# Moving the even-row copies out of PSUM from VectorE to ScalarE in a transformer block's first residual stage

## The chip, the cores and the metric

The kernel runs on the eight cores of one Trainium2 chip. Each core takes one batch element (2048 rows of 1024 numbers) and there is no communication between the cores. The metric is the device time in microseconds of the slowest core; lower is better.

## The reference

One layer with four layer norms, computed for each of eight batch elements (weights shared, the FFN's weights int32 scaled by 1/127, biases zero in the data but applied):

```python
x = x + layernorm(attention(layernorm(x)))      # 16 heads of 64, causal, 2048 x 2048
x = x + layernorm(ffn(layernorm(x)))            # silu(x Wg) * (x Wu), hidden 3072, then Wd
```

## The kernel before

The work of a core comes in this order. (1) The first layer norm of the 16 row tiles of 128 x 1024, with their transposes. (2) Q, K and V projections and causal attention, the projections fed in between the steps of attention. (3) The output projection, L315, with results held feature-major (128 features x 2048 rows, eight such chunks) in `s_f`; ScalarE evicts them from PSUM, L749. (4) The **row stage**, which the change touches: 16 row tiles go through layer norm, residual add and the next layer norm, and back to feature-major. (5) The gate and up matmuls (L840, L851), then the down matmul (L886). (6) A last stage of layer norms, residual adds and stores to memory, which has the same shape as (4).

A tile j of the row stage passes through four functions:

- `p3_A(j)`: TensorE transposes the eight 128 x 128 blocks of the tile into one PSUM bank, in bf16 (L761); the bank is chosen by j % 2. A copy takes the bank to `s_ln` (L768), again one of two halves by j % 2. Then `emit_ln` normalizes it into `s_at`.
- `p3_B(j)`: GpSimd adds the result to the residual `s_x` (L780).
- `p3_C(j)`: `emit_ln` normalizes the sum; its mean was already found in stage (1), so the first reduction is left out.
- `p3_D(j)`: TensorE transposes that (L800) and ScalarE copies it from PSUM into `s_f` (L808).

`emit_ln` is a chain over two engines. VectorE: sum (L239, `p3_A` only), sum of squares (L245, reads its source twice), two 128 x 1 operations (L250, L253). ScalarE: logarithm and exponential for the reciprocal root (L256, L259). VectorE: one 128 x 1 operation (L262). ScalarE: the normalizing pass over 128 x 1024 (L265).

The loop issues the functions skewed: at step t come A(t), B(t-1), C(t-2), D(t-3). Each engine runs its own operations in the order in which they are issued. On ScalarE, step t is thus L256, L259, L265 of A(t), then the same three of C(t-2), then L808 of D(t-3). On VectorE it is L768, L239, L245, L250, L253, L262 of A(t), then L245, L250, L253, L262 of C(t-2). On TensorE it is the transposes of A(t), then those of D(t-3).

All dependencies are tracked by name and become semaphore waits in `emit_all`: for each operation the engine is given one wait instruction for every dependency whose count is higher than the highest it has already waited for, in ascending order:

```python
for d in sorted(o["deps"]):
    ch, val, _ = ops[d]["token"]
    ...
    wait(ch, val)        # skipped when this engine has waited for val or more
```

L808 of tile j names in `war` all transposes that read the four-tile group of `s_f` into which it writes.

Of the kernel before, what the change touches and what calls it, by code (L numbers as in the profile page):

```python
# [26 lines left out]
class Prog:  # L27
# [11 lines left out]
    def op(self, engine, emit, reads=(), writes=(), queue=None, war=(),  # L39
           deps=(), bump=()):  # L40
        idx = len(self.ops)
        dep = set(deps)
        for r in reads:
            e = self.res.get(r)
            if e is not None and e[0] is not None:
                dep.add(e[0])
        for w in tuple(writes) + tuple(war):
            e = self.res.get(w)
            if e is not None:
                if e[0] is not None:  # L50
                    dep.add(e[0])
                dep |= e[1]
        dep.discard(idx)
        self.ops.append({"engine": engine, "emit": emit, "deps": dep,
                         "queue": queue, "token": None})
        for r in reads:
            self.res.setdefault(r, [None, set()])[1].add(idx)
        for w in writes:
            self.res[w] = [idx, set()]
        for w in bump:  # L60
            self.res.setdefault(w, [None, set()])[0] = idx
        return idx
# [59 lines left out]
def build_program(trunc=0, trunc_step=None):  # L122
# [40 lines left out]
    op = P.op  # L163
# [278 lines left out]
    def emit_v_round(c, si):  # L442
# [48 lines left out]
       writes=["vones"])  # L491
# [249 lines left out]
    for c in range(ND):  # L741
# [5 lines left out]
        for si in range(4):  # L747
# [4 lines left out]
               reads=["ps%d" % si, "bo"], writes=["zf_%d_%d" % (c, si)],  # L752
               war=["xnT%d" % (4 * si + k) for k in range(4)])

    def p3_A(j):
        par = j % 2
        bank1 = "ps%d" % (4 + par)
        pb = pO[:, 512 * par:512 * (par + 1)].bitcast(BF16)
        for c in range(ND):
            op("pe",  # L760
               lambda e, c=c, j=j, pb=pb: e.transpose(  # L761
                   pb[:, 128 * c:128 * (c + 1)],
                   s_f[:, S * c + 128 * j: S * c + 128 * (j + 1)], IDT),
               reads=["zf_%d_%d" % (c, j // 4), "cst"],
               writes=([bank1] if c == 0 else []),
               bump=([] if c == 0 else [bank1]))
        ztm = s_ln[:, 1024 * par:1024 * (par + 1)]
        op("dve", lambda e, pb=pb, ztm=ztm: e.tensor_copy(ztm, pb[:, 0:1024]),  # L768
           reads=[bank1], writes=["lnr%d" % par],
           war=["osc0", "osc1"])  # L770
        yn = s_at[:, 1024 * par:1024 * (par + 1)]
        emit_ln(ztm, "lnr%d" % par, yn, "yn%d" % par, pid=j % 4, eng="dve",
                dst_war=("at0",) if j < 2 else (),
                war0=(["rrq0", "rrq1", "onq0", "onq1"] if j == 0 else ()))
# [37 lines left out]
    for t in range(NJ + 3):  # L812
        if t < NJ:
            p3_A(t)
        if 0 <= t - 1 < NJ:
            p3_B(t - 1)
        if 0 <= t - 2 < NJ:
            p3_C(t - 2)
        if 0 <= t - 3 < NJ:
            p3_D(t - 3)  # L820

    for hc in range(NHC):
# [12 lines left out]
        for si in range(4):  # L835
            for kc in range(ND):
# [7 lines left out]
                   reads=["wb%d" % gslot] + ["ynT%d" % (4 * si + k) for k in range(4)],  # L844
                   writes=(["ps%d" % si] if first else []),
                   bump=([] if first else ["ps%d" % si]))
            for kc in range(ND):
# [7 lines left out]
                   reads=["wb%d" % uslot] + ["ynT%d" % (4 * si + k) for k in range(4)],  # L855
                   writes=(["ps%d" % (4 + si)] if first else []),
# [5 lines left out]
               reads=["ps%d" % si], writes=["silu%d" % (si % 2)],  # L862
               war=(("rrq1", "onq1") if (hc == 0 and si < 2) else ()))
# [4 lines left out]
               reads=["silu%d" % (si % 2), "ps%d" % (4 + si)],  # L868
               writes=["h_%d_%d" % (hc, si)],
               war=hwar if si == 0 else ())  # L870

    for c in range(ND):
# [5 lines left out]
           writes=["wd%d_0" % slot, "wd%d_1" % slot], queue="qpool",  # L878
           war=((["wb4", "wb5", "q20", "q21"]
                 + ["nbrow%d" % c2 for c2 in range(ND)]) if c < 2 else ()))  # L880
        for si in range(4):
            for hc in range(NHC):
# [8 lines left out]
                   reads=["wd%d_%d" % (slot, hc // 12), "h_%d_%d" % (hc, si)],  # L891
                   writes=(["ps%d" % si] if first else []),
# [5 lines left out]
               reads=["ps%d" % si], writes=["df_%d_%d" % (c, si)],  # L898
               war=(ALLYNT if (c == 0 and si == 0) else ()))
# [90 lines left out]
```

How the kernel before makes its waits and increments, by code:

```python
        def body(ename, eng):  # L88
            wm = {}
            def wait(ch, val):
                if wm.get(ch, 0) < val:
                    eng.wait_ge(sems[ch], val)
                    wm[ch] = val
            for i in per_eng[ename]:
                o = ops[i]
                if o["queue"] is not None and i in burst_settle:
                    wait(o["queue"], burst_settle[i])
                for d in sorted(o["deps"]):
                    ch, val, _ = ops[d]["token"]
                    if ops[d]["queue"] is not None:
                        val = burst_end_val[d]
                    wait(ch, val)
                inst = o["emit"](eng)
                if o["token"] is not None:
                    ch, val, inc = o["token"]
                    inst.then_inc(sems[ch], inc)
            if ename == "sp":
                for d in sorted(final_deps):
                    ch, val, _ = ops[d]["token"]
                    wait(ch, val)
```

## Time and profile before

| | us |
|---|---|
| median of three runs | 1689.13 |
| lowest and highest | 1688.15, 1689.35 |
| the profiled execution | 1688.57 |
| span of its slowest core, the one shown | 1687.0 |
| spans of all eight cores | 1681.6 to 1687.0 |
| granted TensorE clock, cores' mean | 0.852 to 0.855 |
| busy in the span: TensorE, ScalarE, VectorE, GpSimd | 1220.9, 668.7, 503.4, 226.3 |

A span runs from a core's first to its last instruction. The profiled execution's own time is 1.57 us longer than the longest span; what lies around the span is taken as fixed. Busy times of the engines overlap, so they say nothing by themselves of what sets the end.

### The profile page before, as it was taken

The page shows a single profiled execution, that of the slowest core. Times are in us where ns is not written, and L with a number is a line of the kernel's source. Part 1 is how long each engine was busy: PE and PEld are TensorE (multiplying, and loading weights), DVE is VectorE, ACT ScalarE, POOL GpSimd, SP SyncE. Part 2 cuts the span into 40 slices and gives each one's busy share as a digit, 9 for nine tenths or more (in the row PEclk, how much of TensorE's full clock was granted, in tenths as well). Part 3 has the DMA queues.
Part 4 walks back from the last instruction along what each step waited for, and adds up shares of the span by engine and source line. Part 5 has one row for each costly group of instructions (what it writes and reads, how often), then busy time and mean ns, then how long its engine had stood idle before and what let it go on. Part 6 is the DMA issues. An engine that isn't in the chain of part 4 may idle for free.

```text
span 1687.0 us, 22179 instructions; the slowest of 8 cores (1681.6 to 1687.0 us)
## 1 busy us (share of the span) xinstructions
PE 1220.9 (72%) x5648; PEld 539.1 (32%) x5648; DVE 503.4 (30%) x1074; ACT 668.7 (40%) x1004; POOL 226.3 (13%) x205
## 2 busy tenths in 40 slices
PE   1447777776767777677776932299999999999910
PEld 0123232232323323223222422144444444444410
DVE  4543233231332313233221057711122111000076
ACT  3243554546445464454665335621111111111154
POOL 5202101010110101001000123311111111000022
PEclk9768798897978979798887965599999999999955
DMA  7402100001010010000000300044443446244222
GB/s 87 54 1 19 13 14 7 10 11 13 13 14 10 4 17 10 1 7 7 10 4 7 32 7 0 6 44 40 38 39 38 38 38 62 21 38 38 19 88 112
DMA packets 114632, 43.49 MB, mean 26 GB/s; under 512 B 109264, under 2 KB 109392, under 8 KB 114512
## 3 DMA queue, kind: packets, MB, share of 16 engines
q0 software_dynamic: 111360, 35.66, 19.8%
q1 hardware_dynamic: 2432, 6.29, 1.1%
q8 instruction: 52, 0.85, 0.2%
q14 instruction: 68, 0.56, 0.1%
q10 hardware_dynamic: 720, 0.13, 0.0%
HBM read 63.05 MB, written 8.39 MB: 42 GB/s over the span
## 4 chain that ended last, share of the span: by engine, by line
PE 63%; DVE 17%; ACT 10%; issue 7%; DMA 2%; POOL 1%; DVEq 0%; ACTq 0%; POOLq 0%
PE pS L840 10%; PE pO L851 10%; PE pS L886 10%; PE pS L623 8%; PE pS L377 8%; PE pO L560 7%; DVE s_dmp L245 5%; ACT s_at L646 5%; PE pS L452 3%; DVE s_dmp L239 3%; PE pS L315 3%; ACT s_dmp L509 2%; ACT pO L505 1%; DVE s_at L461 1%; DVE s_b L390 1%
## 5 line engine op out<-in xcount | busy, mean ns | idle before, releaser
L646 ACT ACTIVATE s_at<-pS,s_nB 128x512 bf16<-128x512 f32 (+4 forms) x521 | 349.1, 707 | 313.2 <-PE pS L631 155.0
L623 PE MATMUL pS<-s_b,s_y 128*128 128x512 bf16 (+3 forms) x640 | 227.7, 402 | 30.0 <-ACT s_at L646 13.3
L560 PE MATMUL pO<-s_at,s_b 128*128 128x512 bf16 (+3 forms) x640 | 194.5, 405 | 12.0 <-ACT s_at L646 6.8
L840 PE MATMUL pS<-s_f,s_wb 128*128 128x512 bf16 x768 | 183.2, 382 | 0.0
L851 PE MATMUL pO<-s_f,s_wb 128*128 128x512 bf16 x768 | 181.6, 379 | 0.0
L886 PE MATMUL pS<-s_b,s_wd 128*128 128x512 bf16 x768 | 165.9, 379 | 0.0
L860 ACT ACTIVATE s_dmp<-pS 128x512 bf16<-128x512 f32 x96 | 57.3, 597 | 270.2 <-PE pS L840 270.2
L865 DVE TENSOR_TENSOR s_b<-s_dmp,pO 128x512 bf16<-128x512 bf16 x96 | 66.0, 688 | 270.6 <-PE pO L851 256.4
L377 PE MATMUL pS<-s_f,s_wb 128*128 128x512 bf16 x384 | 126.3, 433 | 18.7 <-ACT s_f L291 10.6
L329 POOL TENSOR_TENSOR s_wd<-s_b 128x512 bf16<-128x512 bf16 x64 | 66.4, 1038 | 402.8 <-DVE s_b L390 358.7
L623 PEld LDWEIGHTS pS<-s_b,s_y 128*128 128x128 bf16 x640 | 69.6, 110 | 125.7 <-issue 90.4
L840 PEld LDWEIGHTS pS<-s_f,s_wb 128*128 128x128 bf16 x768 | 75.5, 98 | 91.3 <-issue 1.7
L851 PEld LDWEIGHTS pO<-s_f,s_wb 128*128 128x128 bf16 x768 | 75.2, 98 | 91.0 <-issue 0.8
L886 PEld LDWEIGHTS pS<-s_b,s_wd 128*128 128x128 bf16 x768 | 75.1, 98 | 90.6
L501 DVE CAST s_ln<-pO 64x1024 bf16<-64x1024 f32 x32 | 38.9, 1216 | 194.6 <-PE pO L560 194.5
L560 PEld LDWEIGHTS pO<-s_at,s_b 128*128 128x128 bf16 x640 | 61.1, 106 | 108.4 <-issue 78.0
L239 DVE TENSOR_SCALAR_CACHE_REDUCE s_dmp<-s_ln 128x1024 bf16<-128x1024 bf16 x32 | 38.9, 1215 | 168.5 <-ACT s_ln L916 166.6
L514 PE MATMUL pO<-s_dmp,s_cst 1*64 1x512 bf16 x32 | 15.5, 486 | 88.5 <-ACT s_dmp L509 88.5
L800 PE MATMUL pO<-s_cst,s_at 128*128 128x128 bf16 x128 | 16.2, 306 | 86.8 <-ACT s_at L265 86.8
L895 ACT ACTIVATE s_f<-pS 128x512 bf16<-128x512 f32 x32 | 19.1, 597 | 148.4 <-PE pS L886 148.4
L631 PE MATMUL pS<-s_cst 128*128 128x128 bf16 x256 | 63.4, 247 | 0.0
L283 PE MATMUL pO<-s_cst,s_ln 128*128 128x128 bf16 x128 | 15.0, 290 | 64.1 <-ACT s_ln L265 64.1
(91 smaller groups left out, 1230.5 us busy)
## 6 DMA issues: line engine op xcount, KB each, us to landing
s_wb<-wg POOLq DMA_DIRECT2D x24, 256.0 KB, 5.0
s_wb<-wu POOLq DMA_DIRECT2D x24, 256.0 KB, 4.6
s_wd<-wd POOLq DMA_DIRECT2D x8, 768.0 KB, 10.3
s_x<-x POOLq DMA_DIRECT2D x16, 256.0 KB, 7.7
y<-s_y SPq DMA_DIRECT2D x8, 512.0 KB, 2.6
y<-s_y POOLq DMA_DIRECT2D x8, 512.0 KB, 3.0
s_wb<-wq POOLq DMA_DIRECT2D x8, 256.0 KB, 5.5
s_b<-s_dmp SPq DMA_DIRECT2D x16, 128.0 KB, 2.2
```

Of the source, the lines that this page charges most:

```text
L239: op("dve", lambda e, mc=mc: e.tensor_scalar(dmp, src_ap, 1.0 / D, 0.0, ALU.mult, ALU.add, accum_out=mc), reads=[src_res], writes=[mres, " ...
L245: op("dve", lambda e: e.scalar_tensor_tensor(dmp, src_ap, 1.0 / D, src_ap, ALU.mult, ALU.mult, accum_out=cell(3)), reads=[src_res], writes ...
L329: op("pool", lambda e, src_ap=src_ap, q2=q2: e.tensor_mul(q2, src_ap, src_ap), reads=[dres], writes=["q2%d" % par])
L377: e.matmul(out, wslot(slot)[:, 128 * kc:128 * (kc + 1)], xfm(kc)[:, 512 * si:512 * (si + 1)], start=first, stop=(kc == ND - 1), skip_group ...
L560: e.matmul(pO[:, q0:q0 + n], s_b[:, V0 + 1040 * j + 65 * h: V0 + 1040 * j + 65 * h + 128], s_at[:, 2048 * par + (q0 - 128 * j): 2048 * par ...
L623: e.matmul(pS[:, 512 * sl:512 * sl + n], kpadv[hp][:, 128 * ktc:128 * (ktc + 1)], q_fm(c)[:, q0:q0 + n], start=True, stop=(not diag), skip ...
L631: lambda e, sl=sl: e.matmul(pS[:, 512 * sl:512 * sl + 128], NEGI, LMSK, start=False, stop=True, skip_group_check=True),
L646: lambda e, src=src, dst=dst, c=c: e.activation(dst, src, AF.Exp, bias=s_nB[:, c:c + 1], scale=QSCALE),
L840: e.matmul(acc_view(si), wslot(gslot)[:, 128 * kc:128 * (kc + 1)], xfm(kc)[:, 512 * si:512 * (si + 1)], start=first, stop=(kc == ND - 1)),
L851: e.matmul(pO[:, 512 * si:512 * (si + 1)], wslot(uslot)[:, 128 * kc:128 * (kc + 1)], xfm(kc)[:, 512 * si:512 * (si + 1)], start=first, sto ...
L865: lambda e, hc=hc, si=si, stg=stg: e.tensor_tensor(s_b[:, S * hc + 512 * si: S * hc + 512 * (si + 1)], stg, pO[:, 512 * si:512 * (si + 1)] ...
L886: e.matmul(acc_view(si), s_wd[:, 3072 * slot + 128 * hc: 3072 * slot + 128 * (hc + 1)], s_b[:, S * hc + 512 * si: S * hc + 512 * (si + 1)] ...
```

## The change

In `p3_A` the copy from the PSUM bank to `s_ln` is issued on ScalarE for even tiles. For odd tiles it stays on VectorE. The operation stands in the same place of the issue order, with the same source, destination and dependencies.

```diff
         ztm = s_ln[:, 1024 * par:1024 * (par + 1)]
-        op("dve", lambda e, pb=pb, ztm=ztm: e.tensor_copy(ztm, pb[:, 0:1024]),
-           reads=[bank1], writes=["lnr%d" % par],
-           war=["osc0", "osc1"])
+        if par == 0:
+            op("act", lambda e, pb=pb, ztm=ztm: e.copy(ztm, pb[:, 0:1024]),
+               reads=[bank1], writes=["lnr%d" % par],
+               war=["osc0", "osc1"])
+        else:
+            op("dve", lambda e, pb=pb, ztm=ztm: e.tensor_copy(
+                ztm, pb[:, 0:1024]),
+               reads=[bank1], writes=["lnr%d" % par],
+               war=["osc0", "osc1"])
```

## Rows read from the trace of the kernel before

**Rows 1.** The page's first line: the span of the slowest core

```profile
span 1687.0 us, 22179 instructions; the slowest of 8 cores (1681.6 to 1687.0 us)
```

**Rows 2.** Windows of the row stage: us, busy by engine, clock, DMA

```profile
980.00:1000.00 20.00, 2.83 (x34) 2.15 (x32) 15.25 (x30) 6.03 (x12) 5.24 (x3) 0.61 0.00 0
...
1020.00:1040.00 20.00, 5.60 (x48) 4.88 (x48) 14.63 (x37) 11.58 (x21) 6.35 (x3) 0.50 0.00 0
1040.00:1060.00 20.00, 5.59 (x48) 4.88 (x48) 14.87 (x37) 11.91 (x19) 6.35 (x3) 0.50 0.00 1
```

**Rows 3.** Groups by line, row stage: form, count, busy us, mean ns, idle

```profile
L265 ACT ACTIVATE s_at<-s_ln,s_st 128x1024 bf16<-128x1024 bf16 x16 | 19.8, 1240 | 6.6 <-DVE s_st L262 6.6
...
L808 ACT COPY s_f<-pO 128x1024 bf16<-128x1024 bf16 x13 | 12.9, 993 | 0.9 <-PE pO L800 0.9
L768 DVE COPY s_ln<-pO 128x1024 bf16<-128x1024 bf16 x16 | 10.9, 681 | 58.3 <-PE pO L761 58.3
```

**Rows 4.** Timeline around tile 6's copy: start us, length us, operation, idle before

```profile
1016.29 1.06 PE L761 MATMUL pO<-s_cst,s_f 128*128 128x128 bf16 x8
...
1020.06 2.12 POOL L780 TENSOR_TENSOR s_x<-s_x,s_at 128x1024 bf16<-128x1024 bf16 x1 [4.91 <-ACT s_at L265]
...
1020.50 0.20 ACT L259 ACTIVATE s_st<-s_st 128x1 f32<-128x1 f32 x1
1020.80 0.21 DVE L262 TENSOR_SCALAR s_st<-s_sx,s_st 128x1 f32<-128x1 f32 x1 [0.70 <-ACT s_st L259]
1020.93 0.68 DVE L768 COPY s_ln<-pO 128x1024 bf16<-128x1024 bf16 x1
1021.11 1.24 ACT L265 ACTIVATE s_at<-s_x,s_st 128x1024 bf16<-128x1024 bf16 x1 [0.41 <-DVE s_st L262]
1021.74 1.22 DVE L239 TENSOR_SCALAR_CACHE_REDUCE s_dmp<-s_ln 128x1024 bf16<-128x1024 bf16 x1
1022.26 0.99 ACT L808 COPY s_f<-pO 128x1024 bf16<-128x1024 bf16 x1
...
1023.07 1.23 DVE L245 SCALAR_TENSOR_TENSOR s_dmp<-s_ln 128x1024 bf16<-128x1024 bf16 x1
...
1024.78 0.20 ACT L256 ACTIVATE s_st<-s_st 128x1 f32<-128x1 f32 x1 [1.53 <-DVE s_st L253]
...
1027.96 0.68 DVE L768 COPY s_ln<-pO 128x1024 bf16<-128x1024 bf16 x1
```

**Rows 5.** Timeline, start of the row stage, tiles 0 and 2

```profile
980.41 0.69 ACT L749 ACTIVATE s_f<-pS,s_bo 128x512 bf16<-128x512 f32 x1 [1.04 <-PE pO L761]
980.87 0.69 DVE L768 COPY s_ln<-pO 128x1024 bf16<-128x1024 bf16 x1 [58.25 <-PE pO L761]
...
981.68 1.22 DVE L239 TENSOR_SCALAR_CACHE_REDUCE s_dmp<-s_ln 128x1024 bf16<-128x1024 bf16 x1
...
991.62 1.24 ACT L265 ACTIVATE s_at<-s_ln,s_st 128x1024 bf16<-128x1024 bf16 x1 [0.41 <-DVE s_st L262]
992.25 1.22 DVE L239 TENSOR_SCALAR_CACHE_REDUCE s_dmp<-s_ln 128x1024 bf16<-128x1024 bf16 x1
993.01 2.12 POOL L780 TENSOR_TENSOR s_x<-s_x,s_at 128x1024 bf16<-128x1024 bf16 x1 [3.87 <-ACT s_at L265]
...
993.58 2.62 DVE L245 SCALAR_TENSOR_TENSOR s_dmp<-s_ln 128x1024 bf16<-128x1024 bf16 x1
```

**Rows 6.** Timeline, ScalarE, the first L808

```profile
1007.08 1.24 ACT L265 ACTIVATE s_at<-s_x,s_st 128x1024 bf16<-128x1024 bf16 x1 [0.41 <-DVE s_st L262]
...
1009.20 1.01 ACT L808 COPY s_f<-pO 128x1024 bf16<-128x1024 bf16 x1 [0.88 <-PE pO L800]
```

**Rows 7.** Timeline, start of the last stage, whose copies are all on ScalarE

```profile
1600.22 1.92 ACT L916 COPY s_ln<-pO 128x1024 bf16<-128x1024 bf16 x2
...
1601.35 1.22 DVE L239 TENSOR_SCALAR_CACHE_REDUCE s_dmp<-s_ln 128x1024 bf16<-128x1024 bf16 x1 [166.61 <-ACT s_ln L916]
```

**Rows 8.** Timeline, the first gate matmuls after the row stage

```profile
1100.37 3.62 PE L840 MATMUL pS<-s_f,s_wb 128*128 128x512 bf16 x8
```

## The prediction, made before the changed kernel ran

> **What bounds the kernel now.** I read three views. The page gives the frame: a span of 1687.0 us [rows 1], in an execution of 1688.57 us. The windows then show that only the stage between about 980 and 1100 us matters here. In it TensorE is busy 2.8 to 5.6 of every 20 us at a granted clock of 0.50 to 0.61, while VectorE is busy 14.6 to 15.3 and ScalarE 6.0 to 11.9 [rows 2]. No engine is full, so this is a chain with waits in it, and the timeline has to say which. The reader should follow VectorE: in the steady part it works through a step in 7.03 us (copy of tile 6 at 1020.93, copy of tile 7 at 1027.96) [rows 4], and has gaps only where it waits for ScalarE's tiny L259. ScalarE, on the other hand, has slack in front of L256, 1.53 us in this step, waiting for VectorE's L253 [rows 4]. TensorE isn't in the chain: tile 6's transposes start at 1016.29 and take 1.06 us, so they are done by 1017.35, 3.6 us ahead of the copy [rows 4]. What follows the stage, the gate matmuls at 1100.37 [rows 8], comes behind the last tile's transposes in TensorE's order, so a longer row stage moves everything after it by the same amount.
>
> **What the change takes off VectorE.** From the copy to the next reduction is 1021.74 - 1020.93 = 0.81 us [rows 4], of which 0.68 us is the copy itself (16 of them, mean 681 ns [rows 3]). Eight copies leave: 8 x 0.81 = 6.5 us, if nothing were put in their place.
>
> **What takes their place.** L239 of the same tile reads what the copy writes, so it now waits for ScalarE. The copy stands in ScalarE's order where it stood in the program: behind L265 of C(t-3) and behind L808 of D(t-4), the last two ScalarE operations of the step before. Neither has anything to do with the tile, but an engine takes its operations in order. Before tile 6's reduction, ScalarE starts that L265 at 1021.11 (0.18 us after VectorE has already started its own copy) and L808 at 1022.26 [rows 4]. The copy comes third.
>
> The trace of before has this very operation in its last stage, L916: 128x1024 bf16 from PSUM to `s_ln`. Two in a row take 1.92 us there, and a single one 1.01 (its group's mean is 1013 ns), so that one starts 0.91 us behind the other; VectorE's reduction follows the end of the first (1600.22 + 1.01 = 1601.23) at 1601.35, 0.12 us later [rows 7]. The other near row is L808, 994 ns [rows 3], a copy with a strided destination; between the two lies 0.02 us, so I take 1.01, the same form.
>
> *A full step (tiles 4, 6, 8, 10, 12, 14).* L808 at 1022.26, copy at + 0.91 = 1023.17, its end at + 1.01 = 1024.18, L239 at + 0.12 = 1024.30. Before, L239 started at 1021.74 [rows 4]. The reduction is 2.56 us later: it loses 3.37 us from where the copy had been and gets 0.81 back. Everything behind L239 on VectorE hangs in one chain (L245, L253, then L256 on ScalarE, L262, and C's sequence), and ScalarE's 1.53 us of slack before L256 doesn't give any back, since L256 waits for VectorE. The odd tile that follows keeps its copy on VectorE and its period. Six times 2.56 = 15.4 us.
>
> *Tile 0.* In front of it stands the last L749 (start 980.41, 0.69 us). Back-to-back ScalarE operations overlap by 0.09 us (L265 takes 1.24 and L808 starts 1.15 behind it [rows 4]), so the copy starts at 981.01, and L239 at 981.01 + 1.01 + 0.12 = 982.14, where it was at 981.68 [rows 5]: 0.46 us.
>
> *Tile 2.* There is no C or D yet; in front stands L265 of tile 1 at 991.62. Copy at 992.77, L239 at 992.77 + 1.01 + 0.12 = 993.90, where it was at 992.25: 1.65 us later [rows 5]. But something is given back. L245 of tile 2 took 2.62 us from 993.58 while GpSimd's L780 ran from 993.01 to 995.13; outside of such an overlap L245 takes 1.23 [rows 4, 5]. Moved 1.65 us, L245 starts at 995.23, 0.10 us after GpSimd is done: 2.62 - 1.23 = 1.39 us less. Net 0.26 us.
>
> The Trainium skill (page "SBUF — State Buffer", section "SBUF: two separate sides") says that GpSimd and a VectorE operation with two SBUF inputs take a shared port pair as an exclusive lock, and the loser waits until the other is done. The trace agrees nearly: L245 ends 1.07 us after L780's end at 995.13, where a full wait would have made it 1.23. By that rule L245 would have ended at 996.36 in place of 996.20 and the giving back would be 1.55 us; the total below would be 0.16 us smaller.
>
> In a full step no new such overlap comes. L780 of the step (1020.06 to 1022.18) was over 0.9 us before L245 at 1023.07 [rows 4] and will be over 3.4 us before it.
>
> *Waits in the sequencer.* The first L808 starts at 1009.20, 2.12 us after the L265 in front of it, not 1.15 [rows 6]. By the rule of `emit_all` it has 33 wait instructions (32 for the transposes of tiles 0 to 3, one for its own), which is 2.12 / 33 = 64 ns each, an estimate. Before, this cost nothing, as no one waits for that L808. Now tile 4's copy stands behind it. But ScalarE's copies of tiles 0 and 2 have waited for the transposes of tiles 0 and 2 already, which covers 24 of the 32; 9 are left, 0.58 us, and are hidden in L265's 1.15. I take 0, with 2.12 - 1.15 = 0.97 us as the upper end if I am wrong in it. The copies' own waits are one for the transposes each, and they have stood complete for 3.6 us.
>
> **The sum.** 15.4 + 0.46 + 0.26 = 16.1 us. Against the profiled execution, 1688.57 + 16.1 = 1704.7. The median of runs is 1689.13, 0.56 us above the profiled one, so 1705.2 us, 0.95% slower. The granted clock changes nothing in this: TensorE is at 0.50 in the stage already, 1.2 GHz, and the gate matmuls start from it, before and after (the first eight take 3.62 us [rows 8]).
>
> **Rivals.**
> *The extra ends come in (slower still).* L245 of tile 2 stays in the overlap, by the 0.10 us on which it hangs: + 1.39; and the first L808 stays late: + 0.97. Both: 18.5 us, 1707.6. Against the one: L780's end is fixed by L265 of tile 1, which doesn't move. For it: a tenth of a microsecond is little. Chance 0.10.
> *Faster: the copy gets hidden.* If ScalarE could take the copy in its slack before L262 of C, when the transposes have long landed, VectorE would lose 0.81 us eight times, and 1.39 at tile 2: up to 7.9 us, 1681.3. It decides at one point: whether the copy ends before VectorE's L262 of C (1020.80 [rows 4]). The slack is there (1.53 us against 1.01), but it is earlier in the order than the copy is. Chance 0.03.
> The Trainium skill's rule on this (page "PSUM — Partial Sum Buffer", section "Engine vs sequencer instructions"), that the queues of ScalarE and VectorE are strictly first in, first out, excludes it; with it this rival has no chance, and all rows above are in issue order.
> *Only L265 in front.* If the copy came before L808, it would start at 1022.26 and L239 at 1023.39, 1.65 us late: six times that with the ends, 10.6 us, 1699.7. It needs another issue order than the diff has. Chance 0.03.
> *No change.* The stage is absorbed behind it, if the first gate weights were what the gate matmuls wait for. But the weights' transfers are queued on GpSimd behind L780 of the last tile and so move with the stage. Chance 0.02; 1689.1.
>
> **How the numbers follow.** The forecast has 0.82. Downward its range has the copy's other row (eight times 0.02 = 0.2 us), the terms of tiles 0 and 2 at nothing (0.7), the runs' spread (1.2) and the profiled execution's distance from the median (0.6): 2.7 us, 1702.5. Upward it has the two extra ends and the spread: 1707.6 + 1.2 = 1708.8. The last three rivals, 0.08, stay outside. A difference of 0.2%, 3.4 us, is about what can be told from none. Slower: 0.82 + 0.10 + 0.03 = 0.95; same 0.02; faster 0.03.
>
> **What would show it.** In the profile after, ScalarE should have a copy of about 1.01 us directly behind L808 at every even tile from 4 on; L239 of these tiles should name that copy as the end of an idle time of about 3.4 us on VectorE; steps should alternate, about 9.6 us into an even tile's copy turn and 7.0 for odd ones; L245 of tile 2 should take 1.23 us; the first L808 should be no longer late. The gate matmuls should start near 1116.5. I am wrong if the steps stay at 7 us, or if VectorE makes up for time after the wait.

## The result, and the profile after

The changed kernel takes 1703.86 us (median of eight runs) against 1688.42 us for the kernel before in the same comparison; the ratio is 1.009, with a 95% interval from 1.0079 to 1.0101. The change makes the kernel about 15.4 us slower. The prediction had 1705.2 us, 16.1 us more than before; of the 1.3 us between 1705.2 and 1703.86, 0.7 us are the kernel before, whose median is 1688.42 here and was 1689.13 when the forecast was made. (In this and the comparisons below, executions in which one half of the chip ran at a clearly lower clock are left out of the ratios, except for three of e4, at 1694 to 1703 us, which were only a little slower and stay in.)

The page of the profiled execution, its first line:

```profile
span 1702.5 us, 22149 instructions; the slowest of 8 cores (1696.4 to 1702.5 us)
```

The windows of the row stage after the change, as in [rows 2] (length, busy time and count for TensorE, its weight loads, VectorE, ScalarE, GpSimd, then clock, DMA share and GB/s):

```profile
980.00:1000.00 20.00, 2.73 (x34) 2.11 (x31) 12.31 (x26) 7.63 (x13) 4.66 (x3) 0.64 0.00 0
1020.00:1040.00 20.00, 4.21 (x37) 3.46 (x34) 11.97 (x33) 10.93 (x18) 4.23 (x2) 0.50 0.00 0
1040.00:1060.00 20.00, 4.55 (x41) 4.11 (x42) 10.17 (x27) 11.90 (x20) 6.35 (x3) 0.50 0.00 0
```

VectorE is busy 10.2 to 12.0 of 20 us in the steady part, where it was at 14.6 to 14.9 [rows 2]. It waits more. For how long and for what is in the groups of the row stage (busy us, mean ns, then idle time before the group and what ended it), the counterpart of [rows 3]:

```profile
L239 DVE TENSOR_SCALAR_CACHE_REDUCE s_dmp<-s_ln 128x1024 bf16<-128x1024 bf16 x16 | 19.5, 1220 | 81.3 <-ACT s_ln L769 80.4
...
L769 ACT COPY s_ln<-pO 128x1024 bf16<-128x1024 bf16 x8 | 8.1, 1008 | 0.0
```

Eight copies of 1008 ns each, none of which ScalarE idled for, and 80.4 us of VectorE's idle time in front of L239 that they ended. (58.5 us of these are the wait for the whole stage to begin, as in front of L768 in [rows 3]; the rest, 21.9 us, is new.) The timeline around tile 6's copy, the counterpart of [rows 4]:

```profile
1024.25 1.24 ACT L265 ACTIVATE s_at<-s_x,s_st 128x1024 bf16<-128x1024 bf16 x1 [0.41 <-DVE s_st L262]
1025.39 0.99 ACT L814 COPY s_f<-pO 128x1024 bf16<-128x1024 bf16 x1
...
1026.28 1.01 ACT L769 COPY s_ln<-pO 128x1024 bf16<-128x1024 bf16 x1
...
1027.41 1.22 DVE L239 TENSOR_SCALAR_CACHE_REDUCE s_dmp<-s_ln 128x1024 bf16<-128x1024 bf16 x1 [3.26 <-ACT s_ln L769]
...
1029.10 1.23 DVE L245 SCALAR_TENSOR_TENSOR s_dmp<-s_ln 128x1024 bf16<-128x1024 bf16 x1 [0.46 <-DVE s_dmp L239]
```

L265 of the step before, then L814 (the old L808) 1.14 us behind it, then the copy 0.89 us behind that, then L239 1.13 us after the copy's start. From L265 to L239 it is 3.16 us; before, it was 1021.74 - 1021.11 = 0.63 [rows 4]. A full step loses 2.53 us. (By the starts of L239, two of which lie 9.57 us apart across such a copy where they were 7.02 to 7.03 apart, it is 2.54 to 2.55.)

To compare the stages themselves I measure the row stage from the first transposes (L761) to the first gate matmul, each on the slowest core: 1100.37 - 980.15 = 120.22 us before, 1116.54 - 980.06 = 136.48 us after, 16.26 us more. In each program six of the eight cores agree on this length within 0.2 us. The other two show up to 0.6 us more, because the record of their first gate matmul is missing (a first group of 7 in place of 8). So it is a finer measure than the whole time, and the experiments below are read with it first. (In e8 the slowest core is one of those two, with 122.67 us; the table has the 122.21 of two of the others.)

### The profile page after: what moved, and what is told of

The parts are those of the page before. It is cut to its first block, busy times and chain, and to the rows that moved or that the text cites. A ratio compares the mean times of both kernels' runs of the same rounds, so it can differ in the third digit from the quotient of the medians.

```text
span 1702.5 us, 22149 instructions; the slowest of 8 cores (1696.4 to 1702.5 us)
## 1 busy us (share of the span) xinstructions
PE 1220.1 (72%) x5648; PEld 539.3 (32%) x5648; DVE 496.9 (29%) x1066; ACT 675.5 (40%) x1012; POOL 226.2 (13%) x205
## 4 chain that ended last, share of the span: by engine, by line
PE 63%; DVE 16%; ACT 11%; issue 7%; DMA 1%; POOL 1%; DVEq 0%; ACTq 0%; POOLq 0%
PE pS L846 10%; PE pS L892 10%; PE pO L857 10%; PE pS L623 8%; PE pS L377 7%; PE pO L560 7%; DVE s_dmp L245 5%; ACT s_at L646 5%; PE pS L452 3%; PE pS L315 3%; DVE s_dmp L239 3%; ACT s_dmp L509 2%; ACT pO L505 1%; DVE s_at L461 1%; DVE s_b L390 1%
## 5 line engine op out<-in xcount | busy, mean ns | idle before, releaser
L377 PE MATMUL pS<-s_f,s_wb 128*128 128x512 bf16 x384 | 123.8, 426 | 19.0 <-ACT s_f L291 10.6
L239 DVE TENSOR_SCALAR_CACHE_REDUCE s_dmp<-s_ln 128x1024 bf16<-128x1024 bf16 x32 | 38.9, 1216 | 248.0 <-ACT s_ln L922 166.6
L256 ACT ACTIVATE s_st<-s_st 128x1 f32<-128x1 f32 x64 | 13.0, 203 | 126.0 <-DVE s_st L253 125.9
```

What stands on the lines that cost most here:

```text
L239: op("dve", lambda e, mc=mc: e.tensor_scalar(dmp, src_ap, 1.0 / D, 0.0, ALU.mult, ALU.add, accum_out=mc), reads=[src_res], writes=[mres, " ...
L377: e.matmul(out, wslot(slot)[:, 128 * kc:128 * (kc + 1)], xfm(kc)[:, 512 * si:512 * (si + 1)], start=first, stop=(kc == ND - 1), skip_group ...
```

## The experiments

The row stage, measured that way, and the ratio of the whole kernel to the kernel before (with its 95% interval):

| kernel | row stage, us | more than before | ratio |
|---|---|---|---|
| before | 120.22 | | |
| after the change | 136.48 | 16.26 | 1.009 (1.0079 to 1.0101) |
| e1: all 16 copies on ScalarE, in place | 155.36 | 35.14 | 1.0203 (1.0189 to 1.0216) |
| e7: the odd tiles instead | 137.74 | 17.52 | 1.0098 (1.0083 to 1.0113) |
| e5: copy ahead of L808 | 130.74 | 10.52 | 1.006 (1.0047 to 1.0072) |
| e4: order changed, all on VectorE | 117.25 | -2.97 | 1.0001 (0.9977 to 1.0025) |
| e2: even copies on ScalarE, a step ahead | 113.52 | -6.70 | 0.9956 (0.9943 to 0.997) |
| e3: all copies on ScalarE, a step ahead | 110.07 | -10.15 | 0.9937 (0.9922 to 0.9953) |
| e6: the change from tile 4 on | 138.54 | 18.32 | 1.0103 (1.0089 to 1.0117) |
| e11: e6 with merged waits | 135.59 | 15.37 | 1.0077 (1.0063 to 1.0091) |
| e8: before with merged waits | 122.21 | 1.99 | 1.0001 (0.999 to 1.0012) |
| e13: e8 with L253 on one tensor | 122.07 | 1.85 | 1.0013 (1.0003 to 1.0023) |
| e12: e3 with L253 on one tensor | 108.68 | -11.54 | 0.9927 (0.9912 to 0.9942) |

### e1: all copies in place. Does the loss grow with the number of copies?

```diff
-        if par == 0:
+        if True:
```

> All 16 copies of the row stage on ScalarE, each in its place in the issue order. Theory (the copy waits behind L265 and L808 of the step before): tiles 4 to 15 cost 12 x 2.56 = 30.7 us, tile 0 0.46, tiles 1, 2 and 3 0.26, 0.26 and 1.66: 33.3 us over the kernel before, ratio 1.0197, and every step of the steady part takes 7.03 + 2.56 = 9.59 us. Rival (the loss comes from alternating between the engines, each hand-over costing once): with all copies on one engine the loss is no larger than that of the eight, 15.4 us, ratio 1.009 or less.

The row stage is 35.1 us longer, and a step takes 9.57 us, as two reductions in a row on VectorE show:

```profile
1039.85 1.22 DVE L239 TENSOR_SCALAR_CACHE_REDUCE s_dmp<-s_ln 128x1024 bf16<-128x1024 bf16 x1 [3.26 <-ACT s_ln L769]
...
1049.42 1.22 DVE L239 TENSOR_SCALAR_CACHE_REDUCE s_dmp<-s_ln 128x1024 bf16<-128x1024 bf16 x1 [3.26 <-ACT s_ln L769]
```

The loss is per copy, with 2.54 us for a full step. An alternation between engines is not what costs: here no copy is left on VectorE to alternate with. The stage is 1.8 us longer than the 33.3 us expected; one L253 of 1.90 us in it makes 1.7 of them, on which e8 below has more.

### e7: the odd tiles instead of the even ones

```diff
-        if par == 0:
+        if par == 1:
```

> The change for the odd tiles instead of the even ones. Theory: tiles 5 to 15 lose 6 x 2.56 = 15.4 us, tile 3 loses 1.66 (only L265 in front of its copy), tile 1 loses 1.66 and gets 1.40 back as its L245 moves behind GpSimd's L780: 17.3 us in the row stage, about 137.5 us in place of 120.24, ratio 1.010. Rival (a cost tied to the bank or the half of s_ln of even tiles): under 5 us.

137.7 us measured, 137.5 expected. VectorE idles 3.27 us before L239 of tiles 5, 7, 9 and on, and 2.35 us for tiles 1 and 3, where only an L265 stands in front. So which half of the buffer and which bank the copy uses doesn't matter.

### e5: the copy ahead of L808. What does each operation in front cost?

The normalizing part of `p3_A` becomes a function of its own, `p3_AL`, and the back-transposes with L808 are issued behind the copy of the next step (in this diff and the next, `p3_A` has only the transposes and the copy):

```diff
-    for t in range(NJ + 3):
+    for t in range(NJ + 4):
         if t < NJ:
             p3_A(t)
+        if 0 <= t - 4 < NJ:
+            p3_D(t - 4)
+        if t < NJ:
+            p3_AL(t)
...
-        if 0 <= t - 3 < NJ:
-            p3_D(t - 3)
```

> The eight copies on ScalarE with the copy issued ahead of L808 of the step before, and behind its L265 (the back-transposes and L808 are issued one place later). Theory: the copy starts 0.89 to 0.91 us earlier, a full step loses 1.65 us in place of 2.56: 6 x 1.65 + 0.46 + 0.26 = 10.6 us over before, ratio 1.0063, and VectorE idles 2.3 to 2.4 us before L239 of even tiles. Rival (L808 isn't what the copy waits for): 15.4 us as with the change, ratio 1.009.

10.5 us in the row stage, 10.6 expected, and the order of the rows is the one asked for:

```profile
1037.96 1.24 ACT L265 ACTIVATE s_at<-s_x,s_st 128x1024 bf16<-128x1024 bf16 x1 [0.41 <-DVE s_st L262]
1039.11 0.99 ACT L769 COPY s_ln<-pO 128x1024 bf16<-128x1024 bf16 x1
...
1040.00 1.01 ACT L818 COPY s_f<-pO 128x1024 bf16<-128x1024 bf16 x1
...
1040.22 1.22 DVE L239 TENSOR_SCALAR_CACHE_REDUCE s_dmp<-s_ln 128x1024 bf16<-128x1024 bf16 x1 [2.35 <-ACT s_ln L769]
```

L265, the copy (L769) 1.15 us behind it, and the old L808 (L818 here) behind the copy; VectorE idles 2.35 us. So of the 3.26 us that VectorE waits in the changed kernel, L808 makes 0.91. What is left is the end of L265, the copy itself and 0.1 us of hand-over. L808 itself lost nothing by its later place: it runs while VectorE is already at work.

### e2 and e4: the copy a step ahead, and its control

Now only the place is changed, seen from the reader of the copy. The transposes and the copy of tile t are issued in front of the layer norm of tile t-1, with everything behind them one step later:

```diff
-    for t in range(NJ + 3):
+    for t in range(NJ + 4):
         if t < NJ:
             p3_A(t)
         if 0 <= t - 1 < NJ:
-            p3_B(t - 1)
+            p3_AL(t - 1)
         if 0 <= t - 2 < NJ:
-            p3_C(t - 2)
+            p3_B(t - 2)
         if 0 <= t - 3 < NJ:
-            p3_D(t - 3)
+            p3_C(t - 3)
+        if 0 <= t - 4 < NJ:
+            p3_D(t - 4)
```

e2 has the change's copies (even tiles on ScalarE), e4 has all of them on VectorE.

> The same eight copies on ScalarE, but each tile's transposes and copy are issued one step ahead of its layer norm (the loop becomes transposes and copy of t, layer norm of t-1, add of t-2, second norm of t-3, back-transposes of t-4). Theory (only the place in ScalarE's order costs): the copy ends in the slack before L256, VectorE loses 0.81 us in eight steps, of which ScalarE gives back about 0.10 each by starting L256 late: 5 to 6 us faster than before, ratio 0.9965 to 0.997, with no idle time of VectorE before L239. Rival (a copy on ScalarE costs by itself, by its length or the hand-over to VectorE): still slower than before, ratio over 1.003.

> Control: the loop order of e2_ahead_even with all copies left on VectorE. Theory: nothing is taken off VectorE, the chain has the same operations per step, so within 1 us of the kernel before, ratio 0.9995 to 1.0005. Rival (the new order itself gains): as fast as e2_ahead_even.

e2 is faster than the kernel before, 0.9956 where the change gave 1.009, with the same eight copies on the same engine. This tells the theory from its rival: a copy on ScalarE isn't dear by itself. What made it dear was that VectorE's next operation read it. In the timeline of e2 around a step with a copy on ScalarE:

```profile
1037.85 1.21 DVE L239 TENSOR_SCALAR_CACHE_REDUCE s_dmp<-s_ln 128x1024 bf16<-128x1024 bf16 x1
...
1039.18 0.99 ACT L818 COPY s_f<-pO 128x1024 bf16<-128x1024 bf16 x1
...
1040.07 1.01 ACT L769 COPY s_ln<-pO 128x1024 bf16<-128x1024 bf16 x1
...
1040.97 0.21 ACT L256 ACTIVATE s_st<-s_st 128x1 f32<-128x1 f32 x1
...
1044.15 0.68 DVE L773 COPY s_ln<-pO 128x1024 bf16<-128x1024 bf16 x1
...
1044.75 1.21 DVE L239 TENSOR_SCALAR_CACHE_REDUCE s_dmp<-s_ln 128x1024 bf16<-128x1024 bf16 x1
```

L239 starts with no idle time before it, for its tile was copied a step ago. On ScalarE the copy still stands behind the normalizing L265 and the back-copy (L818 here) and in front of L256, as in the change; but it is the copy of the next tile, and what VectorE does next doesn't read it. The copy (L769) falls where ScalarE had its 1.53 us of slack in [rows 4] and ends just as L256 comes, which starts 0.90 us behind the copy's start without ScalarE having idled. From one L239 to the next it is 6.90 us where a copy on VectorE lies between them and 6.21 where none does, in place of 7.03 twice.

In e4 I was wrong by about 3 us: I had expected no change from the order alone. The stage is 2.97 us shorter, and seven of the ten executions that count lie at 1683.8 to 1685.0 us, about 4 us below the kernel before. With the other three the ratio by itself can't tell it from 1. The rows of VectorE show where the gain in the stage comes from:

```profile
1047.98 0.68 DVE L768 COPY s_ln<-pO 128x1024 bf16<-128x1024 bf16 x1
1048.58 1.21 DVE L239 TENSOR_SCALAR_CACHE_REDUCE s_dmp<-s_ln 128x1024 bf16<-128x1024 bf16 x1
...
1054.79 0.68 DVE L768 COPY s_ln<-pO 128x1024 bf16<-128x1024 bf16 x1
1055.39 1.21 DVE L239 TENSOR_SCALAR_CACHE_REDUCE s_dmp<-s_ln 128x1024 bf16<-128x1024 bf16 x1
```

From the copy to the next reduction it is 0.60 us, in place of 0.81 [rows 4]. That reduction (of tile t-1) doesn't read what the copy (of tile t) writes. In the old order it does, and so waits for the copy's end on its own engine, by a semaphore wait that `emit_all` puts there: 0.21 us. Fifteen such pairs make 3.1 us. At the start of the stage two larger effects come on top and nearly cancel: the copies of tiles 2 and 3 now wait 1.5 us each for the L265 of two tiles before, which reads the half of `s_ln` that they write, and the two L245 that took 2.6 us each beside GpSimd's add (the one of tile 2 is in [rows 5]) take 1.25. The copy of tile 2 in e4:

```profile
987.13 0.69 DVE L768 COPY s_ln<-pO 128x1024 bf16<-128x1024 bf16 x1 [1.51 <-ACT s_at L265]
```

In the prediction I had put 0.81 us as what a copy takes off VectorE; 0.2 us of it is a wait for the result, which another order gets rid of as well. Of e2's 6.7 us, 8 x 0.2 = 1.6 come from this on the odd tiles, and the rest, less 0.09 us for each copy by which ScalarE starts L256 late, from the eight copies that left VectorE.

### e3: all copies on ScalarE, a step ahead

> All 16 copies on ScalarE, issued one step ahead as in e2_ahead_even. Theory (ScalarE takes the copy at no cost as long as it ends in the slack before L256): VectorE has no copy left, a step takes 6.2 to 6.3 us against 6.81 and 6.21 in turn in e2_ahead_even and 7.03 before; 14 steps x 0.73 = 10 us faster than before, ratio about 0.994. Rival (ScalarE becomes the bound with a copy in each step, as in e1_all_in_place): steps of 7 us or more, ratio 1.00 or over.

A step takes 6.30 us, 10.2 us less in the row stage, ratio 0.9937:

```profile
1035.04 1.21 DVE L239 TENSOR_SCALAR_CACHE_REDUCE s_dmp<-s_ln 128x1024 bf16<-128x1024 bf16 x1
...
1036.37 0.99 ACT L818 COPY s_f<-pO 128x1024 bf16<-128x1024 bf16 x1
...
1037.26 1.01 ACT L769 COPY s_ln<-pO 128x1024 bf16<-128x1024 bf16 x1
...
1038.16 0.21 ACT L256 ACTIVATE s_st<-s_st 128x1 f32<-128x1 f32 x1
...
1041.34 1.21 DVE L239 TENSOR_SCALAR_CACHE_REDUCE s_dmp<-s_ln 128x1024 bf16<-128x1024 bf16 x1
```

ScalarE takes 16 copies of 1 us at the price of 0.09 us a step (6.30 against the 6.21 of e2); in e1 it took the same 16, behind the same two operations, for 35 us.

### e6 and e11: wait instructions in front of the first L808

```diff
-        if par == 0:
+        if par == 0 and j >= 4:
```

and e11 has, besides, one wait per semaphore in `emit_all`:

```diff
+                top = {}
                 for d in sorted(o["deps"]):
...
-                    wait(ch, val)
+                    top[ch] = max(top.get(ch, 0), val)
+                for ch in top:
+                    wait(ch, top[ch])
```

> The change for tiles 4, 6, 8, 10, 12 and 14 only; tiles 0 and 2 keep their copy on VectorE. Theory of the wait instructions: the first L808 again has 33 of them, starts about 0.97 us late as before the change, and tile 4's copy stands behind it, so VectorE idles 3.26 + 0.97 = 4.2 us before L239 of tile 4 and 3.26 before the other five: 6 x 2.56 + 0.97 = 16.3 us over before. Also L245 of tile 2 takes 2.62 us again. Rival (the first L808 was late for another reason, or its lateness doesn't pass on): 3.3 us before tile 4 too, 15.4 us over before.

> As e6_from_tile4, with one wait instruction for each semaphore, on the highest count needed, in place of one for every dependency (in the whole kernel, and the same conditions are waited for). Theory: the first L808 has one wait and follows L265 by 1.15 us, VectorE idles 3.3 us before tile 4, the row stage is 0.97 us shorter than in e6_from_tile4. Rival: tile 4 as in e6_from_tile4, 4.2 us. The time of the whole kernel also holds what the merged waits do elsewhere, see e8_one_wait.

ScalarE in e6, then in e11 (where L268, L817 and L772 are L265, L808 and the copy); in each the L265 in front, the first L808 and tile 4's copy:

```profile
1005.35 1.24 ACT L265 ACTIVATE s_at<-s_x,s_st 128x1024 bf16<-128x1024 bf16 x1 [0.41 <-DVE s_st L262]
1007.48 1.01 ACT L814 COPY s_f<-pO 128x1024 bf16<-128x1024 bf16 x1 [0.89 <-PE pO L806]
1008.39 1.02 ACT L769 COPY s_ln<-pO 128x1024 bf16<-128x1024 bf16 x1
```

```profile
1006.00 1.24 ACT L268 ACTIVATE s_at<-s_x,s_st 128x1024 bf16<-128x1024 bf16 x1 [0.41 <-DVE s_st L265]
1007.15 0.99 ACT L817 COPY s_f<-pO 128x1024 bf16<-128x1024 bf16 x1
1008.04 1.01 ACT L772 COPY s_ln<-pO 128x1024 bf16<-128x1024 bf16 x1
```

With 33 waits L808 comes 2.13 us behind L265, with one it comes 1.15 behind. VectorE idles 4.27 us before tile 4's L239 in e6, 3.26 before the others. The row stage of e11 is 15.37 us longer than before, which is 6 x 2.56 within 0.01 us. So the prediction's reading of the 2.12 us in [rows 6] holds: (2.13 - 1.15) us is what the waits add, and what the row names as the end of the idle time (a back-transposition, L800) was not its cause. It also shows why the change itself paid nothing for it: the copies of tiles 0 and 2 had passed 24 of these waits ahead of time, and nine are left in front of that operation (33 and 9 are counted from the programs). In the changed kernel the first L814 is 1.15 us behind its L265, and not late:

```profile
991.97 1.24 ACT L265 ACTIVATE s_at<-s_ln,s_st 128x1024 bf16<-128x1024 bf16 x1 [0.41 <-DVE s_st L262]
993.12 0.99 ACT L769 COPY s_ln<-pO 128x1024 bf16<-128x1024 bf16 x1
993.35 2.12 POOL L786 TENSOR_TENSOR s_x<-s_x,s_at 128x1024 bf16<-128x1024 bf16 x1 [3.87 <-ACT s_at L265]
994.23 1.22 DVE L239 TENSOR_SCALAR_CACHE_REDUCE s_dmp<-s_ln 128x1024 bf16<-128x1024 bf16 x1 [2.35 <-ACT s_ln L769]
...
995.56 1.22 DVE L245 SCALAR_TENSOR_TENSOR s_dmp<-s_ln 128x1024 bf16<-128x1024 bf16 x1
...
1007.65 1.24 ACT L265 ACTIVATE s_at<-s_x,s_st 128x1024 bf16<-128x1024 bf16 x1 [0.41 <-DVE s_st L262]
1008.80 0.99 ACT L814 COPY s_f<-pO 128x1024 bf16<-128x1024 bf16 x1
...
1009.69 1.01 ACT L769 COPY s_ln<-pO 128x1024 bf16<-128x1024 bf16 x1
...
1010.82 1.22 DVE L239 TENSOR_SCALAR_CACHE_REDUCE s_dmp<-s_ln 128x1024 bf16<-128x1024 bf16 x1 [3.26 <-ACT s_ln L769]
```

The first five of these rows are tile 2 in the changed kernel: L239 at 994.23, GpSimd's add from 993.35 to 995.47, L245 at 995.56, just behind it, with 1.22 us in place of 2.62 [rows 5]. In e6, where tile 2 stays on VectorE, L245 takes 2.62 us again.

e6 is 2.0 us longer than 16.3, however. An L253 in it takes 1.94 us, where 0.16 is usual.

### e8, e13 and e12: the long L253

e8 is the kernel before with the merged waits alone.

> The kernel before with the merged waits of e11_from_tile4_one_wait. Theory: nothing in the row stage beyond 0.3 us, since the late L808 is waited for by nobody there; in attention eight operations of VectorE (L526) have more than eight wait instructions each and TensorE waits for them in the trace of before (4.0 us, eight times), so 1 to 5 us faster, ratio 0.997 to 0.9995. Rival (wait instructions cost nothing where an engine has other work queued): ratio 0.9995 to 1.0005.

The whole kernel does not change (0.999 to 1.0012), so the gain in attention that I expected isn't there. And the row stage gets 2.0 us longer, 1.8 of them by one operation:

```profile
1024.83 1.23 DVE L248 SCALAR_TENSOR_TENSOR s_dmp<-s_x 128x1024 bf16<-128x1024 bf16 x1 [0.24 <-issue]
...
1026.14 2.12 POOL L783 TENSOR_TENSOR s_x<-s_x,s_at 128x1024 bf16<-128x1024 bf16 x1 [4.97 <-ACT s_at L268]
1026.29 1.97 DVE L256 TENSOR_TENSOR s_st<-s_st 128x1 f32<-128x1 f32 x1
```

L256 (the old L253) subtracts two 128x1 tensors, 0.16 us elsewhere. Here it takes 1.97 and ends at 1028.26, when GpSimd's add does (1026.14 + 2.12). In the steady part of the kernel before, GpSimd's add starts 0.11 us after this operation has started (1027.08 and 1026.97 in the step behind that of [rows 4]). Here a gap of 0.24 us on VectorE ahead of L248, for which the trace names no cause, has moved the operation 0.15 us behind the add's start. In e6 a gap of 0.40 us does the same. The kernel before has such a gap too, 0.46 us before its L253 at 1060.00, and the changed kernel has one (the last of the rows of tile 6 above), each at a place where it hits nothing. e3 shows it in both directions:

```profile
985.47 1.23 DVE L245 SCALAR_TENSOR_TENSOR s_dmp<-s_ln 128x1024 bf16<-128x1024 bf16 x1
...
985.72 2.95 POOL L790 TENSOR_TENSOR s_x<-s_x,s_at 128x1024 bf16<-128x1024 bf16 x1 [18.82 <-ACT s_at L265]
...
986.93 1.75 DVE L253 TENSOR_TENSOR s_st<-s_st 128x1 f32<-128x1 f32 x1
```

GpSimd's add takes 2.95 us in place of 2.12, since L245 is running when it wants to start; and L253 then takes 1.75, until 988.68, GpSimd's end at 988.67.

That fits what the Trainium skill says (page "SBUF — State Buffer", section "SBUF: two separate sides"): an exclusive lock between GpSimd and a VectorE operation with two SBUF inputs, held for the whole instruction. The trace agrees here nearly, with both sides waiting, for a VectorE operation of one element per lane too: GpSimd's add (2.12 us) ends 1.97 us after L245's end at 986.70, and L253 (0.16 us) ends with the add, so both come some 0.15 us sooner than a full wait gives. By the rule, an L253 with one tensor input would not wait, unless it ran in one of the modes that use both ports. Two kernels test that:

```diff
-        op("dve", lambda e: e.tensor_tensor(s_st[:, b + 4:b + 5], cell(3),
-                                            cell(4), ALU.subtract),
+        op("dve", lambda e: e.tensor_scalar(s_st[:, b + 4:b + 5], cell(3),
+                                            cell(4), None, ALU.subtract),
```

> e8_one_wait with the same edit of L253. Theory: the L253 of 1.97 us in its row stage (122.2 us, against 120.24 before) is gone and the stage is back at 120.0 to 120.8 us; the whole is 1 to 2 us faster than e8_one_wait, ratio 0.999 to 1.000. Rival (the merged waits themselves made the stage longer): 122 us.

> e3_ahead_all with L253, the 128x1 subtraction, written as an operation with one tensor and a scalar operand (as L250 and L262 are) in place of two tensors. Theory (L253 stands still while GpSimd's residual add runs, since both its inputs are tensors in SBUF): the two L253 of 1.75 us at the start of the row stage in e3_ahead_all fall to 0.2, at most 0.05 us more for each of the other 30: row stage 2 to 3 us shorter than the 110.1 us of e3_ahead_all, ratio about 0.992. Rival (the long L253 only shows a wait that something else sets): a long operation stays at the same place, within 0.5 us of e3_ahead_all.

The long L253 is gone in both. In e12 two of them (at 987.50 and 991.33 us) run for 0.21 us in the middle of an add of 2.95 us. The group in e12, row stage:

```profile
L253 DVE TENSOR_SCALAR s_st<-s_st 128x1 f32<-128x1 f32 x32 | 6.8, 214 | 3.4
```

32 of them in 6.8 us: none stands out, at a mean of 214 ns. But it was 160 ns with two tensors, and 32 x 0.054 is 1.7 us. In e13 all of that is in the chain (a step takes 7.14 us in place of 7.03): it gains 0.1 us over e8 in the stage, one long one (1.8) less 1.7. The ratios show no gain in the whole either, 1.0013 against 1.0001; my 120.0 to 120.8 us was wrong, as I had priced the edit by the long one and not the 31 others. In e12 a steady step is only 0.06 us longer than in e3, since the copy on ScalarE delays L256 there anyway. Two long ones are 3.2 us less; 1.3 us go to the other L253, and 0.5 to a new collision, an L245 that now comes while GpSimd's add still runs:

```profile
992.37 1.77 DVE L245 SCALAR_TENSOR_TENSOR s_dmp<-s_x 128x1024 bf16<-128x1024 bf16 x1
```

That leaves the 1.4 us by which the row stage of e12 is shorter than that of e3; the ratios of the two, 0.9927 and 0.9937, don't tell them apart. So the cause of the long L253 is shown; the edit pays in e3's order, where two of them go, and not in e8, where one does.

## Why the prediction was right, point by point

**Where the kernel is bound.** Right. The row stage grew by 16.26 us, and the span by 15.5. The gate matmuls start at 1116.54, where the prediction had 1116.5.

**A full step, 2.56 us.** Measured 2.53 from L265 to L239 in the changed kernel and 2.54 to 2.55 by L239's period, 2.54 in e1. The parts hold: L808 0.91 of it (e5), and the copy behind L265 1.65 (e5, e7). The idle time named as a sign was about 3.4 us and is 3.26; 3.37 was the distance from the old copy's start, while VectorE is still at work on an L262 at that point, so its wait is shorter.

**Tile 0, 0.46 us.** From the first transposes to L239 it was 981.68 - 980.15 = 1.53 [rows 5] and is 982.02 - 980.06 = 1.96: 0.43.

**Tile 2, 1.65 us less 1.39.** From L265 to L239 2.26 us, before 0.63: 1.63, and L245 shorter by 1.40. The 0.10 us on which it hung held (995.56 against 995.47).

**The first L808's waits at nothing.** Right, and e6 and e11 show the other case at 0.98 us.

**No change behind the row stage.** Right in size, not quite in fact. The stages behind it became 0.7 us shorter. The first gate matmuls in the changed kernel:

```profile
1116.54 2.89 PE L846 MATMUL pS<-s_f,s_wb 128*128 128x512 bf16 x8
...
1119.26 1.89 PE L857 MATMUL pO<-s_f,s_wb 128*128 128x512 bf16 x8
```

They take 2.89 us, where before the first eight took 3.62 [rows 8] and the next eight were still slow in part. I had said that this start is the same before and after. From 990 us on the granted clock is 0.50 to the end of the stage in both. It rises after the gate matmuls begin: before, it is still 0.50 in the microsecond up to 1104, which ends 3.6 us after the first of them; after, it is 0.72 in the one from 1118, which begins 1.5 us after the first. Before, six cores take 3.62 us for the first eight; in the changed kernel's execution one core does and five take 2.9 (the record of the other two cores lacks one of the eight). Gate and up together take 332.52 us in place of 333.34, down 165.76 in both, the last stage 87.68 in place of 87.53. In e5 gate and up take 333.59, in e3 333.80, and these are executions with shorter row stages than the changed kernel's; no order was tried that moves only this, so what sets the moment stays open. It was worth under 1.3 us in these four executions, and it makes most of the difference between the 16.3 us of the row stage and the 15.4 of the whole.

The sum of the measured parts is 6 x 2.545 + 0.43 + 0.23 = 15.9 us of the 16.26, with a step taken by L239's period. A late L256 in the changed kernel, 0.28 us at about 1066.7, is another. It was not foreseen and no row names its cause. So the closeness of 16.1 and 16.26 is in part luck: the parts that were forecast make 15.9. In the whole kernel's 15.4 us the 0.7 us gained behind the stage then goes the other way.

**The rival "only L265 in front"** had the price 10.6 us, and e5, which makes that order, has 10.5. **The rival "hidden"** had 7.9 us as its end. It didn't come in the order of the change, where each copy stands directly in front of its reader. With another issue order (e2) 6.7 us came, and by e4 partly for another reason than I gave.

## What to carry to other kernels

Moving an operation to an engine with idle time pays only if its result is not needed before that idle time begins. Look up what stands in front of it and what waits for it: here 16 copies cost 35 us when VectorE's next reduction read them and won 10 us when it read the copy of a step before, with the same copies behind the same operations on ScalarE. Issue a hand-over between engines one step ahead of its reader; in this kernel, whose every dependency is a semaphore wait, that paid even on one engine (e4). And when an edit shifts a chain, check the small operations at the edge of another engine's long one.

## What the runs showed of the hardware that I had not expected

- A VectorE operation that reads the result of the one in front of it starts 0.81 us after the start of a copy of 0.68 us, with a semaphore wait on that copy between them; one whose wait was met long before starts 0.60 us after it (e4).
- A 128x1 subtraction of two tensors takes 0.16 us, and 1.75 to 1.97 us when GpSimd's 2.1 us add is under way (e1, e2, e3, e6, e8). With a scalar operand it takes 0.21 us, and none of 64 was long (e12, e13).
- 33 wait instructions whose conditions are long met put 2.13 us between two ScalarE operations (e6), where one puts 1.15 (e11) and nine also 1.15 (the changed kernel). An estimate from this is 0.06 us each, hidden as long as their sum is under 1.15. Merging the waits in the whole kernel (2375 to 1512 of ScalarE's alone, counted from the program) left its time within 0.12% (e8, ratio 0.999 to 1.0012).
